# First attention group by rows: queries and values made beside the keys, half of the low halves on GpSimd, four key units moved ahead of the steps, image 1 loaded in single pieces

## The reference, cut to what matters

```python
x = x + attention(_gn(x))      # _gn: group normalisation over 32 groups
x = x + experts(_gn(x))        # 4 experts of width 96, the best 2 of each token

def attention(x):              # 12 heads of 32
    q, k, v = split(x @ qkv_w.T + qkv_b)
    reg_k, reg_v = registers @ qkv_w[384:].T + qkv_b[384:]      # 16 registers
    scores = q . concat(k, reg_k) / sqrt(32), masked to a 7 x 7 neighbourhood (registers always seen)
    return (softmax(scores) . concat(v, reg_v)) @ out_w.T + out_b
```

## Time and profile before

| | |
|---|---|
| median of 3 runs | 632.62 us (629.4 to 635.39) |
| profiled execution, own time | 633.32 us |
| its span, first to last instruction | 631.4 us (1.9 us lie around it) |
| busy: PE, DVE, ACT, POOL | 557.0, 435.6, 312.5, 301.4 us |
| PE's granted clock, mean | 0.966 of full speed |
| steps begin (step 0, 1, 2, 4) | 72.4, 87.2, 98.9, 122.5 us |
| PE sits idle for the maxima's DMA | 5.25 us ahead of step 1, 5.67 us ahead of step 13 |

### The profile page before, as it was taken

How to read it: one execution, slowest core, us unless ns; L and a number is a source line. 1 busy time by engine, 2 the same in 40 slices (tenths; PEclk the granted TensorE clock), 3 DMA queues, 4 the chain that set the end, 5 groups by cost and what they waited for, 6 DMA issues and landing times.

```text
span 631.4 us, 22435 instructions
## 1 busy us (share of the span) xinstructions
PE 557.0 (88%) x9227; PEld 390.8 (62%) x9227; DVE 435.6 (69%) x1071; ACT 312.5 (49%) x622; POOL 301.4 (48%) x442
## 2 busy tenths in 40 slices
PE   3567969999999869999999999996988589998996
PEld 2344746767677646777677767774665346664553
DVE  6784559887976658678977898668795558763332
ACT  1762534447767624444444444556664438744321
POOL 4105746885387712556579713465554232313221
PEclk8697989999999979999999999999899799999999
DMA  9858979566866598756876588666520011211122
GB/s 309 194 140 218 277 238 219 172 174 156 198 182 167 164 320 202 206 152 182 203 186 184 156 205 210 161 175 193 128 61 6 2 38 38 77 41 54 57 76 75
DMA packets 130988, 97.79 MB, mean 155 GB/s; under 512 B 66684, under 2 KB 123944, under 8 KB 130888
## 3 DMA queue, kind: packets, MB, share of 16 engines
q1 hardware_dynamic: 120456, 73.84, 44.6%
q0 software_dynamic: 10432, 22.52, 11.5%
HBM read 59.83 MB, written 35.68 MB: 151 GB/s over the span
## 4 chain that ended last, share of the span: by engine, by line
PE 62%; DVE 17%; DMA 6%; issue 5%; POOL 4%; ACT 3%; SPq 2%; DVEq 0%; POOLq 0%; ACTq 0%
PE ps L1177 41%; PE ps L1309 5%; PE ps L1328 5%; PE ps L1331 4%; PE ps L1279 3%; DMA QS<-MT 3%; DVE MX L609 2%; DVE ST L511 2%; DVE KU L579 1%; DVE XH L603 1%; DMA X<-in_x 1%; DVE GT_ L549 1%; DVE KT L588 1%; PE ps L1294 1%; PE ps L1450 1%
## 5 line engine op out<-in xcount | busy, mean ns | idle before, releaser
L984 ACT ACTIVATE PT<-ps 128x448 f32<-128x448 f32 (+1 forms) x207 | 96.2, 508 | 99.0 <-PE ps L1309 98.8
L609 DVE TENSOR_REDUCE MX<-ps 128x2 f32<-128x372 f32 x216 | 106.8, 535 | 14.0 <-PE ps L1279 13.9
L1177 PE MATMUL ps<-X,WQ 128*128 128x384 f16 x486 | 89.8, 333 | 2.5 <-POOL X L377 1.6
L491 POOL TENSOR_TENSOR KT<-QS,KT 128x384 f16<-128x384 f32 x36 | 34.3, 961 | 94.6 <-ACT KT L1094 94.6
L1328 PE MATMUL ps<-PT,VR 128*32 128x112 f32 (+1 forms) x1656 | 76.6, 259 | 0.0
L1177 PE MATMUL ps<-OS,WO 128*128 128x384 f16 x324 | 70.2, 327 | 5.9 <-POOL OS L419 3.7
L1331 PE MATMUL ps<-PT,SELW 128*32 128x112 f32 (+1 forms) x1656 | 74.0, 253 | 0.0
L1177 PE MATMUL ps<-XH,WQ 128*128 128x384 f16 x324 | 62.4, 342 | 8.6 <-DVE XH L559 7.9
L1309 PE MATMUL ps<-QS,KB 122*128 122x112 f16 (+1 forms) x864 | 59.4, 213 | 11.5 <-DMA QS<-MT 11.2
L1177 PEld LDWEIGHTS ps<-X,WQ 128*128 128x128 f16 x486 | 46.1, 100 | 30.8 <-issue 4.3
L1279 PE MATMUL ps<-KB,QS 120*32 120x186 f16 x1728 | 56.8, 246 | 8.5 <-DMA QS<-qscr 5.2
(11 more groups left out here) (182 smaller groups left out, 1068.3 us busy)
## 6 DMA issues: line engine op xcount, KB each, us to landing
KB<-kscr SPq DMA_DIRECT2D x108, 192.0 KB, 3.8
kscr<-KT SPq DMA_DIRECT2D x36, 384.0 KB, 5.1
VR<-vscr SPq DMA_DIRECT2D x216, 56.0 KB
QS<-qscr SPq DMA_DIRECT2D x108, 96.0 KB, 3.9
qscr<-QT POOLq DMA_DIRECT2D x36, 192.0 KB, 3.7
X<-in_x SPq DMA_DIRECT2D x6, 576.0 KB, 7.0
vscr<-VT POOLq DMA_DIRECT2D x54, 64.0 KB, 2.4
vscr<-WR POOLq DMA_DIRECT2D x54, 64.0 KB, 2.7
```

Of the source, the lines that this page charges most:

```text
L491: nc.gpsimd.tensor_tensor(HW[:, m % 2, 1, k, :], HF[:, unit % 2, :], HW[:, m % 2, 0, k, :], ALU.subtract).then_inc(s_["hl"], 1)
L609: V.tensor_reduce(out=MX[:, g % 2, t, 2 * pair:2 * pair + 2], in_=ps[:, S_BANK(i), 0:2 * RUN].rearrange("p (h n) -> p h n", h=2), op=ALU.m ...
L984: A(PTS[pt_slot(n)][:, 0:w], ps[:, ST_BANK(n), 0:w], ACT.Exp, scale=SCORE).then_inc(s_["exd"], 1)
L1177: last = mm(bank, lhsT(a, k), rhs(b, k), start=(k == 0 and n == 0), stop=(finish and k == steps - 1 and n == 2))
```

## The change

Group 0's queries and values are made by rows too. `FIRST` becomes a list of units for each strip: keys and queries of a strip together, values from strip 2 on, the last three values at the end. The queries' unit takes the 64 tokens of the strip in each of the six tiles, so its buffer is written to `qscr` in pieces of 128 bytes (768 before), by SP and not by POOL, two DMAs for each strip (`first_queries_out`, `q_first`). A unit of values takes a block of 16 rows and 3 tiles. PSUM banks go round six instead of four.

In the first stage DVE computes all three values `GT_` of a strip and one low half; POOL computes the other two (`POOL_K[0]`), and copies the registers' keys into the buffers one by one between them. `weights_low(0)` moves ahead of `parameters`; ACT's `registers_high(0, 0)` moves ahead of the first normalised strip.

The scores of steps 0 and 1 no longer have group 0's units between them; four key units of group 1 (`EARLY`) stand there instead. Steps 0 to 3 then have two units each, not three (`fillers`, `PART`); steps 4 and 5 and all other groups keep three. In SP's queue the keys-out of these four units stand between `queries_in(1)` and step 0's own entries, each behind a wait for its unit.

Image 1's first load goes out in steps 0, 1 and 2, one piece in the second and one in the last third, the first behind that step's `maxima_in`; its second load in steps 12 to 17, one piece a step, behind `maxima_in`.

```diff
-FIRST = (("q", 0), ("q", 1), ("v", 0), ("v", 1), ("q", 2), ("v", 2), ("q", 3), ("v", 3), ("q", 4), ("v", 4), ("q", 5), ("v", 5))
-NEXT = ((("k", 0), ("k", 1), ("k", 2)), (("k", 3), ("k", 4), ("k", 5)), (("q", 0), ("q", 1), ("v", 0)),
-        (("v", 1), ("q", 2), ("v", 2)), (("q", 3), ("v", 3), ("q", 4)), (("v", 4), ("q", 5), ("v", 5)))
+FIRST = ((("k", 0), ("q", 0)), (("k", 1), ("q", 1)), (("k", 2), ("q", 2), ("v", 0)), (("k", 3), ("q", 3), ("v", 1)),
+         (("k", 4), ("q", 4), ("v", 2)), (("k", 5), ("q", 5)), (("v", 3), ("v", 4), ("v", 5)))
+FLAT = sum(FIRST, ())
+ORDER = (("k", 0), ("k", 1), ("k", 2), ("k", 3), ("k", 4), ("k", 5), ("q", 0), ("q", 1), ("v", 0),
+         ("v", 1), ("q", 2), ("v", 2), ("q", 3), ("v", 3), ("q", 4), ("v", 4), ("q", 5), ("v", 5))
+EARLY = 4
+PART = (EARLY, 6, 8, 10, 12, 15)
+
+
+def fillers(g):
+    gi, s = divmod(g, 6)
+    if gi == 5:
+        return (None, None, None)
+    at, to = (PART[s], (PART + (18,))[s + 1]) if gi == 0 else (3 * s, 3 * s + 3)
+    return (ORDER[at:to] + (None, None))[0:3]
+
+
 SECOND_STATS = {1: (2, 1, 1), 2: (2, 2, 1), 3: (2, 2, 1), 4: (2, 1, 1)}
 MEANS = {5: 1, 27: 2}
...
-POOL_K = ((), (0, 1, 2), (0, 1, 2), ())
+POOL_K = ((0, 1), (0, 1, 2), (0, 1, 2), ())
@@ -264,7 +279,7 @@
 
             def keys_out(gi, a):
                 sp.wait_ge(s_["k_lo"], 6 * gi + a + 1)
-                sp.wait_ge(s_["krg"], 3 * gi + 3)
+                sp.wait_ge(s_["krg"], 3 * gi + min(a, 2) + 1)
@@ -281,7 +296,11 @@
 
             def queries_in(g):
                 gi, s = divmod(g, TILES)
-                sp.wait_ge(q_out[s], 16 * (gi + 1))
+                if g == 0:
+                    for i in range(STRIPS):
+                        sp.wait_ge(q_first[i], 32)
+                if gi:
+                    sp.wait_ge(q_out[s], 16 * gi)
                 if g >= TILES:
                     sp.wait_ge(s_["st_mm"], 6 * (g - 5))
...
+
+            def first_queries_out(a):
+                sp.wait_ge(s_["q_lo"], a + 1)
+                for part in range(2):
+                    sp.dma_start(tile_rows(qscr[part])[:, :, a * 64:(a + 1) * 64], tile_rows(QT[:, a % 2, part, :])).then_inc(q_first[a], 16)
 
             for a in range(STRIPS):
                 keys_out(0, a)
+                first_queries_out(a)
             sp.wait_ge(s_["t_in"], 16 * 5)
             keys_in(0)
             queries_in(0)
             keys_in(1)
             queries_in(1)
+            keys_out(1, 0)
             values_in(0)
+            keys_out(1, 1)
             keys_in(2)
             queries_in(2)
+            for a in range(2, EARLY):
+                keys_out(1, a)
             for g in range(LAST):
...
                     keys_in(g + 3)
                     queries_in(g + 3)
-                if gi < STAGES - 1:
-                    for kind, i in NEXT[s]:
-                        if kind == "k":
-                            keys_out(gi + 1, i)
...
-            queries_out(0, 0)
-            queries_out(0, 1)
+            for a in range(STRIPS):
+                for k in POOL_K[0]:
+                    low_half(0, a, k)
+                if a < 3:
+                    register_keys_of(0, a)
+                if a > 1:
+                    for kind, i in FIRST[a - 1]:
+                        if kind == "v":
+                            values_out(0, i)
             for half in range(2):
                 register_values(0, half)
-            values_out(0, 0)
-            values_out(0, 1)
-            for s in (2, 3):
-                queries_out(0, s)
-                values_out(0, s)
-            queries_out(0, 4)
+            values_out(0, 3)
+            register_keys(1)
             values_out(0, 4)
+            values_out(0, 5)
             maxima_in(0)
-            queries_out(0, 5)
-            values_out(0, 5)
-            register_keys(1)
...
                         register_keys(gi + 2)
-                    if g == 0:
-                        for half in range(2):
-                            at = half * 3 * SN
-                            pool.dma_start(raw1(p, at, 3 * SN), x[1, :, p, at:at + 3 * SN]).then_inc(x_in[1][p][half], 16)
-                    if g == 2 * TILES:
-                        pool.wait_ge(s_["v_mm"], 6 * KC)
-                        for half in range(2):
-                            at = half * 3 * SN
-                            pool.dma_start(xs(1, p, at, 3 * SN), x[1, :, p, at:at + 3 * SN]).then_inc(x_re[2 * p + half], 16)
                     if p == 1 and g + 1 < LAST:
                         maxima_in(g + 1)
+                    if g < KC and p:
+                        at = (p - 1) * 3 * SN
+                        pool.dma_start(raw1(g, at, 3 * SN), x[1, :, g, at:at + 3 * SN]).then_inc(x_in[1][g][p - 1], 16)
+                    if gi == 2 and p == 1:
+                        if s == 0:
+                            pool.wait_ge(s_["v_mm"], 6 * KC)
+                        at = s % 2 * 3 * SN
+                        pool.dma_start(xs(1, s // 2, at, 3 * SN), x[1, :, s // 2, at:at + 3 * SN]).then_inc(x_re[s], 16)
@@ -648,51 +687,53 @@
             link(last)
             aggregate()
             group_copy(0, 7, 0)
+            weights_low(0)
             parameters(0, 7, 0)
             more_parameters(0)
             dve.wait_ge(s_["b16"], 1)
 
+            def low_of(gi, kind, i):
+                if kind == "k":
+                    keys_low(gi, i)
+                if kind == "q":
+                    queries_low(gi, i)
+
             for a in range(STRIPS):
-                for k in range(2):
+                for k in range(KC):
                     normalised(0, a, k)
-                if a == 0:
-                    weights_low(0)
-                for k in range(KC):
-                    low_half(0, a, k)
+                low_half(0, a, 2)
                 if a == 0:
                     register_low(0, 0)
-                if a:
-                    keys_low(0, a - 1)
+                else:
+                    for unit in FIRST[a - 1]:
+                        low_of(0, *unit)
             keys_low(0, STRIPS - 1)
-            queries_low(0, 0)
-            queries_low(0, 1)
             weights_low(1)
-            queries_low(0, 2)
+            queries_low(0, STRIPS - 1)
             weights_low(2)
-            for i in (0, 1):
-                maximum(0, i)
-            queries_low(0, 3)
             V.scalar_tensor_tensor(out=WO[:, 1, :, :].rearrange("p k n -> p (k n)"), in0=raw_o, scalar=WS,
                                    in1=WO[:, 0, :, :].rearrange("p k n -> p (k n)"), op0=ALU.mult, op1=ALU.subtract
                                    ).then_inc(s_["wolo"], 1)
             dve.wait_ge(s_["bvhi"], 1)
             V.tensor_tensor(BVH[:, 1, :], cols["bv"], BVH[:, 0, :], ALU.subtract).then_inc(s_["bvlo"], 1)
-            for i in (2, 3, 4, 5):
...
             dve.wait_ge(s_["bv_mm"], 1)
             V.scalar_tensor_tensor(out=cols["obx"], in0=ps[:, 6, 0:KC], scalar=1 / WS, in1=cols["ob"],
                                    op0=ALU.mult, op1=ALU.add).then_inc(s_["obx"], 1)
+            for p in range(3):
+                for i in (2 * p, 2 * p + 1):
+                    maximum(0, i)
+                if p < EARLY:
+                    low_of(1, *ORDER[p])
+            split_maxima(0)
+            for p in range(3):
+                for i in (2 * p, 2 * p + 1):
+                    maximum(1, i)
+                if KC + p < EARLY:
+                    low_of(1, *ORDER[KC + p])
+            split_maxima(1)
 
...
             deviation(0)
+            def evict(gi, kind, i):
+                {"k": keys_high, "q": queries_high, "v": values_out}[kind](gi, i)
+
+            registers_high(0, 0)
             for a in range(STRIPS):
-                for k in range(2):
+                for k in range(KC):
                     normalised(0, a, k)
-                third_value(0, a)
-                normalised(0, a, 2)
-                if a == 0:
-                    registers_high(0, 0)
                 if a:
-                    keys_high(0, a - 1)
+                    for unit in FIRST[a - 1]:
+                        evict(0, *unit)
             keys_high(0, STRIPS - 1)
-            queries_high(0, 0)
-            queries_high(0, 1)
             weights_high(1)
-            values_out(0, 0)
-            values_out(0, 1)
-            queries_high(0, 2)
+            queries_high(0, STRIPS - 1)
             weights_high(2)
-            values_out(0, 2)
-            queries_high(0, 3)
+            evict(0, *FIRST[STRIPS][0])
             act.wait_ge(s_["wo_in"], 16)
             A(WO[:, 0, :, :].rearrange("p k n -> p (k n)"), raw_o, ACT.Copy, scale=WS).then_inc(s_["wohi"], 1)
             A(BVH[:, 0, :], cols["bv"], ACT.Copy).then_inc(s_["bvhi"], 1)
-            values_out(0, 3)
-            queries_high(0, 4)
-            values_out(0, 4)
+            for unit in FIRST[STRIPS][1:]:
+                evict(0, *unit)
+            for g in (1, 2):
```

(84 more changed lines are left out.)

128 lines of the change are left out of this document (56 added, 72 removed).

## The result

Measured over 20 runs each, the changed kernel takes 636.53 us (median, 631.11 to 646.17) and the kernel before 631.35 (628.53 to 635.39): ratio 1.0063, 95% interval 1.0034 to 1.0092. The ratio leaves out the two slowest executions of the changed kernel (642.28 and 646.17), which are more than 1.5% above its fastest; the other 18 have a median of 635.5. The forecast was 615.8 us. The change is a little slower where I had forecast 2.7% faster.

What follows compares the result with a forecast made beforehand. PE was taken as the bound from step 0, with holes in the first stage, before the scores and in steps 1 and 13. Terms +2.4 - 11.8 - 7.6 = -17.0 from 633.32 gave 616.3, median 615.8; range 610 to 623.

Steps and rivals of the forecast that it cites:

- Holes at the maxima: Starts of steps 1 and 13: PE's waits for the maxima's DMA go, worth 7.15 and 7.6 us.
- the one for image 1's pieces: Image 1's loads in pieces behind the maxima: new placing costs nothing in steps 12 to 17, at most 1 us stalls early.
- its companion for steps 0 to 3: Steps 0 to 3: 36.9 us plus 1.0 plus 0.4 for SP's tight queue, 38.3 in all, a gain of 11.8.
- The rival of loads and queue: Steps 0 to 3: pieces in flight or SP's queue delay maxima, statistics or scores; 4 us given back, 620; chance 0.13.
- the gain does not appear: Steps 1 and 13: pieces meet steady traffic and the holes only move to later steps; 628 us; chance 0.04.
- a whole queue of six ahead: Steps 1 and 13: both holes have six pieces queued ahead of them, so the gain's not appearing was called unlikely.
- Head: First stage and scores up to step 0: step 0 begins at 74.8, 2.4 us later than before; bounds 71 to 80.
- the scores' start: End of the first stage: first scores start at 59.2, about five us late, with all 18 units done, not 12.
- the score phase: Scores of steps 0 and 1: 18.5 us less two units of 1.49 gives 15.5, taken as 15.6.
- The early units' saving in the steps: Steps 0 to 3: two units instead of three, so four units of 1.49 leave, 6.0 us of PE.
- The rival of the 128-byte pieces: Query strips written to DRAM: small pieces land so slowly that the scores wait; 639 at 8 us a strip; chance 0.04.

Runs made afterwards that it cites:

- the last pair of runs: Changed kernel, all low halves on VectorE, first load in the first stage's strips, second thinned over steps 12 to 20: ratio 0.9924 without early units, 0.9979 with.

## Why the prediction was wrong

Holes at the maxima: right in kind. Both stalls on `QS<-MT` vanished, as the forecast said, and step 13's was worth 5.5 of its 7.6 us. For step 1 the credit is not the pieces': with both loads in bulk the changed kernel has no such stall either, since its maxima go out 5 us behind the pieces.

The step that failed is the one for image 1's pieces, "I cost the new placing at nothing", with its companion for steps 0 to 3, where 0.4 us stood for lateness in SyncE's queue. I asked only whether the *maxima* would be late again. The maxima had waited behind DMA engines that were full: 1.01 busy from the start of step 0 to the end of the hole at 87 us, and 0.82 over steps 0 to 3, in the trace before. Spreading the same bytes over steps 0 to 2 leaves the work, and the next customer waits: keys for the scores, in step 2 (5.15 us and half clock behind it). The kernel before with only the pieces shows it without the rest of the change, 53.3 us for steps 0 to 3 against 50.1, and taking the bytes away from there brings 42.8. The one unit fewer in each of these steps did not pay in full meanwhile: 4.3 us for four units in the changed kernel (51.4 against 47.2), 6.0 with the load away. That every due time came 1.5 us earlier would explain it; no run separates that. Of 8.9 us missed in steps 0 to 3, 5.9 go when the load goes (41.3 in its absence), 3 remain: there step 0 lasts 10.7 us, partly at half clock, and step 2 begins with 1.93 us of wait for the maxima.

The rival of loads and queue had this mechanism with 4 us and 0.13. The rival "the gain does not appear" had it with the time nearest to the result, 628, and 0.04; I had argued it away with "a whole queue of six ahead" of the maxima, though four pieces stood there in step 0. I had the row, 0.94 busy in step 2, and used it as a caution and not as a sum. The sum would have been: 0.82 of 50 us is 41 us of full transfer, more than the 38.3 that I gave these steps. (In the changed kernel it is 0.87 of 47.2, again 41 us.) It would have been a warning and not a price: the same sum says nothing against steps 12 to 17, where spreading kept 4.3 us.

Head: forecast +2.4, measured +7.6 at step 0. 3.1 us of the error are the scores' start (62.3, not 59.2), and 2.4 of these are GpSimd's low halves, by the run without them. I had sized contention on GpSimd's side, from its 1.96 us, and taken VectorE's own operations at the undisturbed price. The stretched engine was VectorE, three values 1.85 (3.14 in one strip) where I had taken 1.3, and a low half 1.08 where I had taken 0.5. The Trainium skill's rule on this contention (GPSIMD Engine Reference, Key points) agrees with these rows, and I used it for one of two sides. 2.1 us are the score phase, 17.7 and not 15.6. I had subtracted two units' PE time from the old phase; but a key unit between scores is a chain (PE, ACT, VectorE, then the next unit through the same bank), and PE waited 0.9, 0.9, 1.79 and 2.07 us on VectorE. Without the units it is 10.8.

Step 0 by the prediction's sum is 8.1 (14.83 less the hole of 5.25 and a unit of 1.49) and took 11.5: the waits just named left PE at the half clock when it began (0.74 granted over the step). I had priced half clock behind the scores' start only.

The early units' saving in the steps: right with the first load away (6.0 us in the last pair of runs, 4.3 with it in place), and smaller than the 8.2 and 7.8 us that they add ahead of step 0.

The sum, in the trace: 5.2 us in the head, 8.9 in steps 0 to 3 and 2.1 behind step 14 are 16.2, against the 15.9 between the 17.0 forecast and the 1.1 gained there. One slip of mine is small: 616.3 less 0.7 is 615.6, not 615.8.

The rival of the 128-byte pieces, with the Trainium skill's least size for line rate (DMA: Bandwidth & Descriptors, Specifications): the trace agrees that they are slower, by 0.7 us of landing, and the run without them shows no time gained for this kernel.

What stays open: the changed kernel's trace is 1 us shorter than the trace before, and its median 4 us above the median before. Its 18 executions in the ratio spread over 8.5 us with a median 3.1 above the profiled one, those of the kernel before over 7 with a median 2.0 below its own. No trace here is of one of the changed kernel's longer runs, so the forecast's miss is accounted for in the trace and these last 5 us are not.

## What to carry to other kernels

Before spreading a burst of transfers, add up the DMA share over the whole stretch where it shall go, and name everyone who waits for a transfer there, not only the one that waits now. In steps 0 to 3 (0.82 busy) two pieces a step moved the hole to the next customer; in steps 12 to 17 (0.79 to 0.83) one piece a step kept most of the gain. The sum alone did not decide, and neither did room: in the kernel before, the first stage went from 0.53 to 1.05 busy with the load in it, and the scores came 0.7 us later. Changing the order only changed who was late.

Work moved into another phase is priced by that phase's chain and not by the engine that it frees: four units saved 6.0 us in the steps at best and cost 6.9 in the score phase. When a second engine takes over a part of a job, price what the first one's remaining instructions become beside it.

## What the runs showed of the hardware

GpSimd beside VectorE, with GpSimd on two-input subtractions of 128 x 384 (fp32 and 16-bit in): VectorE's own such subtraction takes 1.08 us instead of 0.56. Of its three plain scale-and-adds of the same size (0.47 each alone) the third, which runs beside GpSimd's work, takes 1.07, and in one strip 2.36. GpSimd's subtraction takes 1.03 (median) instead of 0.91, and in the strip of the 2.36 it is not slowed at all (1.79 for two). The sharing cost VectorE far more than GpSimd: 4.62 us a strip against 4.24 with all low halves on VectorE.

Writing 768 pieces of 128 bytes lands in 3.5 us and 128 pieces of 768 bytes in 2.8 (96 KB each): the sixfold number of pieces costs 0.7 us, and 0.12 of DMA share between 44 and 56 us (0.96 against 0.84).

One DMA issue of 56 KB on SyncE's queue takes 0.65 us (median). Beside or right behind image 1's first load single ones took 2.57 and 1.77 us (changed kernel, at 91.21 and 94.55) and 3.46 (before, at 86.86).
